# Down projection of an expert layer from the f32 product, in place of two f16 halves of it

## The chip, the cores and the metric

One core of a Trainium2 chip. The metric is the device time in microseconds, median of the runs. The engines are PE (TensorE), DVE (VectorE), ACT (ScalarE), POOL (GpSimd) and SP (SyncE); SP and POOL mostly issue DMAs here, each from a queue of its own that runs in order.

## The reference

Eight rows (batch entries) of 512 tokens with 128 features. Attention with a sine in place of the softmax, 16 heads of 8, then a mixture of experts: one shared expert and eight routed ones, two of which each token uses.

```python
x = x + attention(layernorm(x))            # logits/scale, sin(30 * logits), times V, times Wo
h = layernorm(x)
expert(h, Wg, Wu, Wd) = (silu(h @ Wg.T) * (h @ Wu.T)) @ Wd.T      # 128 -> 256 -> 128
out = x + expert(h, shared) + sum over the top 2 of 8 of score * expert(h, e)
```

All arrays are f32.

## The kernel before

The program is a hand-written order of *slots*, numbered a. Rows 0 to 7 of attention take 32 slots each (0 to 255); from slot 256 (`TAIL`) on only expert work is left, up to slot 331. Each engine runs its own loop over the slots and does in each slot what `plan()` and the slot lists give it. In a slot of attention PE computes the scores of two heads (`scores`), in even slots it multiplies sines with the values (`sum_values`), and ACT takes the sine (`sine`). The projections of the next row and the transposes of the last one lie in slots of their own.

Expert work comes in 148 *tiles* of 128 tokens: 32 *shared* ones, 84 *sparse* ones (tokens of rows 0 to 6 sorted by expert, in four groups of rows, g = 0 to 3) and 32 *full* ones (row 7, each expert over all its tokens). Below slot 256 a tile starts every second slot, after it in every slot. A tile i goes through these steps:

- `gate_up` on PE at `GU_SLOT`: 12 f16 matmuls of 128x128 (high and low halves of weights and tokens, three products for each of four blocks). Up to tile 79 they write the one bank `g_ps`, and so wait for `hidden` of the tile before; later there are three banks.
- `silu` on ACT and `hidden` on DVE at `HID_SLOT` (one slot later, from slot 256 on the same slot). `hidden` writes `hid` in f32 and then casts it to `hid_hi` in f16.
- `hidden_lo` on POOL in the same slot: `hid` minus `hid_hi`, to `hid_lo` in f16.
- `down` on PE at `D_SLOT`, 6 slots after `GU_SLOT` (4 from slot 254 on): 6 f16 matmuls of 128x128 after a wait for `hid_lo`. In a slot PE does `down` before `gate_up`.
- `read_down` on DVE in the same slot, ahead of that slot's `hidden`. A shared or full tile is added to `x_all`. A sparse tile is copied to one of three `y_sb`, which waits for the store of the sparse tile three before, and SP stores it (`store_y`) one slot later.

POOL has the scatters and gathers too. `scatter` sends the tokens of a group to `x_sorted` (16 DMAs for a group of two rows, one a slot, from slots 91, 155, 219; 8 from slot 251). `gather` fetches the results from `y_sorted`, again one DMA a slot, from slots 174, 238, 288 and 318; the first of a group waits until every y of the group is stored. Ten slots after the first gather DVE's `combine` adds the first row of the group (slots 184, 248, 298, 328); the second follows eight slots later or more.

SP's loop does for a slot first `load_rows` (a DMA transpose for a sparse tile, five tiles ahead at most), then `load_weights` (384 KB for a sparse tile, six ahead at most), `load_full` (the weights of an expert for row 7; two buffers, so it waits for the last `down` of the expert two before), then `store_y`, and then the loads and stores of queries and keys. For groups 1 and 2 the first five `load_rows` lie in slots 172 and 236 and wait for the group's scatters; the last y of the group before (tiles 34 and 65) is stored by SP in these same slots, behind them.

The weights are split once at the start (`weights_hi` on POOL, `split_weights` on DVE), stored to `w_dram` and fetched from there.

Of the kernel before, what the change touches and what calls it, by code (L numbers as in the profile page):

```python
# [7 lines left out]
ALU = mybir.AluOpType  # L8
ACT = mybir.ActivationFunctionType
AX = mybir.AxisListType  # L10
F32 = mybir.dt.float32
# [4 lines left out]
P = 128  # L16
# [35 lines left out]
WCOLS = 2 * HID + CH * DM  # L52
TO_WHOLE = 1.5 * 2.0 ** 23
# [35 lines left out]
WR, WF, XT, HR, HB = 6, 2, 5, 5, 6  # L89
# [49 lines left out]
def down_slots():  # L139
    out = []  # L140
    for a in GU_SLOT:
        a = a + 6 if a < TAIL - 2 else a + 4
        out.append(max(a, out[-1]) if out else a)
    return out
# [112 lines left out]
def sine_attention_moe_kernel(nc, x, wq, bq, wk, bk, wv, bv, wo, bo, wgu, wd, wr, rb, ident, out):  # L257
    with ExitStack() as ctx:
# [12 lines left out]
        def dram(name, shape, dt):  # L271
# [34 lines left out]
        w_shared = sb("w_shared", [P, 2 * WCOLS], F16)  # L306
        w_ring = [sb(f"w_ring{i}", [P, 2 * WCOLS], F16) for i in range(WR)]
        w_full = [sb(f"w_full{i}", [P, 2 * WCOLS], F16) for i in range(WF)]
# [3 lines left out]
        hid_hi = [sb(f"hid_hi{i}", [P, HID], F16) for i in range(HB)]  # L312
        hid_lo = [sb(f"hid_lo{i}", [P, HID], F16) for i in range(HB)]
# [24 lines left out]
        w_dram = dram("w_dram", (ROUTED, P, 2 * WCOLS), F16)  # L338
# [28 lines left out]
        gu_done, gate_ready, hid_ready, hid_hi_ready, hid_lo_ready, down_done, d_read = (  # L367
            sem(n) for n in ("gu_done", "gate_ready", "hid_ready", "hid_hi_ready", "hid_lo_ready", "down_done", "d_read"))
# [176 lines left out]
        def _(pe):  # L545
# [116 lines left out]
            def gate_up(i):  # L662
# [7 lines left out]
                else:  # L670
# [7 lines left out]
                    hi, lo = (x2_t[row % 2][:, half * SEQ + t * P:half * SEQ + (t + 1) * P] for half in range(2))  # L678

# [5 lines left out]
                for c in range(2 * CH):  # L685
                    here = bank[:, c * P:(c + 1) * P]
                    w_hi, w_lo = w[:, c * P:(c + 1) * P], w[:, WCOLS + c * P:WCOLS + (c + 1) * P]
# [5 lines left out]
            def down(i):  # L693
# [5 lines left out]
                pe.wait_ge(hid_lo_ready, i + 1)  # L699
# [4 lines left out]
                here = d_bank(i)  # L704
                for c in range(CH):
                    hi, lo = (half[i % HB][:, c * P:(c + 1) * P] for half in (hid_hi, hid_lo))
                    col = 2 * HID + c * DM
                    w_hi, w_lo = w[:, col:col + DM], w[:, WCOLS + col:WCOLS + col + DM]
                    pe.matmul(here, hi, w_hi, start=(c == 0), stop=False)  # L709
                    pe.matmul(here, hi, w_lo, start=False, stop=False)  # L710
                    mm = pe.matmul(here, lo, w_hi, start=False, stop=(c == CH - 1))  # L711
# [164 lines left out]
        def _(dve):  # L876
# [190 lines left out]
            def hidden(i):  # L1067
                dve.wait_ge(gate_ready, i + 1)
                if i >= HR:
                    dve.wait_ge(hid_lo_ready, i - HR + 1)  # L1070
# [275 lines left out]
```

## Time and profile before

| | us |
|---|---|
| median of 3 runs | 589.16 (585.47 to 592.48) |
| the profiled execution | 589.47 |
| its span | 587.6 |
| attention slots, up to slot 256 | about 447 |
| experts alone, from there to the end | about 140 |

The mean granted clock of PE is 0.919 of full speed. Busy time is the time in which an engine had an instruction of its own under way; waits and DMA issues on SP's and POOL's queues are read from the timelines and from the chain that ended last.

### The profile page before, as it was taken

What the parts mean: (1) busy time and instruction counts of PE and PEld (TensorE: products, weight loads), DVE (VectorE), ACT (ScalarE), POOL (GpSimd) and SP (SyncE); (2) the same over time, 40 slices, a digit from 0 to 9 for tenths busy, and PEclk for the clock granted to TensorE, in tenths of its full rate; (3) what the DMA queues carried; (4) which work ended last, traced back from release to release, by engine and by line L of the source; (5) the groups of instructions that cost most, each with busy time, mean ns of one, the idle gap of its engine ahead of it and who ended that gap; (6) DMA issues with size and microseconds to landing.
All of it is one profiled execution on the core that took longest, in us unless ns stands there. A gap on an engine that the chain in (4) does not pass through costs nothing.

```text
span 587.6 us, 13375 instructions
## 1 busy us (share of the span) xinstructions
PE 462.9 (79%) x4616; PEld 244.4 (42%) x4616; DVE 293.9 (50%) x1040; ACT 327.7 (56%) x455; POOL 259.3 (44%) x317
## 2 busy tenths in 40 slices
PE   3298997998969799889876998789758778666761
PEld 2121233233324344444432444344334777565760
DVE  5424444236324446474634555435454865557852
ACT  2279897797856577567643766656734212221220
POOL 4512212003831322168376322357277733388663
PEclk9689999899989999899977999979978879989986
DMA  2889798162718767874397769933645866677322
GB/s 68 240 205 273 234 294 223 64 171 71 240 41 200 181 201 183 243 208 129 80 227 184 178 187 250 183 110 99 131 117 162 198 167 176 188 222 205 99 63 54
DMA packets 101715, 99.14 MB, mean 169 GB/s; under 512 B 32272, under 2 KB 82832, under 8 KB 101648
## 3 DMA queue, kind: packets, MB, share of 16 engines
q1 hardware_dynamic: 95376, 88.91, 56.6%
q0 software_dynamic: 3584, 7.35, 4.9%
q10 hardware_dynamic: 2688, 2.03, 1.2%
q8 instruction: 37, 0.61, 0.5%
q14 instruction: 30, 0.25, 0.2%
HBM read 60.63 MB, written 32.11 MB: 158 GB/s over the span
## 4 chain that ended last, share of the span: by engine, by line
PE 26%; issue 16%; DMA 15%; POOL 15%; SPq 13%; DVE 10%; ACT 5%; ACTq 1%; POOLq 0%; DVEq 0%
PE o_ps L606 6%; PE score L593 5%; SPq L447 5%; POOL x_sorted L1252 5%; POOL y_back L1263 5%; DMA y_sorted<-y_sb 4%; POOL hid_lo L1244 3%; DVE hid L1071 3%; DMA w_ring<-w_dram 3%; PE g_ps L688 2%; DVE x_all L1108 2%; ACT gate L811 2%; PE g_ps L690 2%; PE g_ps L689 2%; SPq L420 2%
## 5 line engine op out<-in xcount | busy, mean ns | idle before, releaser
L790 ACT ACTIVATE attn<-score 128x1024 f32<-128x1024 f32 x256 | 256.4, 1026 | 133.9 <-PE score L593 131.2
L1244 POOL TENSOR_TENSOR hid_lo<-hid,hid_hi 128x256 f16<-128x256 f32 x148 | 102.4, 693 | 204.2 <-DVE hid_hi L1076 203.3
L606 PE MATMUL o_ps<-attn,vals 128*32 128x512 f32 x1024 | 143.3, 633 | 0.1
L593 PE MATMUL score<-queries,keys 64*128 64x512 f16 x512 | 101.7, 404 | 16.2 <-DMA queries<-q_four 9.4
L1071 DVE SCALAR_TENSOR_TENSOR hid<-g_ps,gate 128x256 f32<-128x256 f32 x103 | 43.4, 422 | 128.2 <-ACT gate L811 122.1
L593 PEld LDWEIGHTS score<-queries,keys 64*128 64x128 f16 x512 | 23.9, 93 | 138.9 <-issue 74.6
L688 PE MATMUL g_ps<-xt,w_ring 128*128 128x128 f16 x256 | 51.1, 232 | 24.7 <-DVE hid L1071 10.8
L811 ACT ACTIVATE gate<-g_ps 128x256 f32<-128x256 f32 x103 | 39.2, 381 | 37.7 <-PE g_ps L690 28.6
L689 PE MATMUL g_ps<-xt,w_ring 128*128 128x128 f16 x256 | 51.2, 233 | 0.0
L690 PE MATMUL g_ps<-xt,w_ring 128*128 128x128 f16 x256 | 51.1, 233 | 0.0
L1076 DVE CAST hid_hi<-hid 128x256 f16<-128x256 f32 x148 | 47.3, 320 | 5.1
L811 ACT ACTIVATE gate<-score 128x256 f32<-128x256 f32 x45 | 17.3, 384 | 55.8 <-PE score L690 40.4
L688 PEld LDWEIGHTS g_ps<-xt,w_ring 128*128 128x128 f16 x256 | 26.8, 105 | 31.7 <-issue 27.6
L709 PE MATMUL d_ps<-w_ring,hid_hi 128*128 128x128 f16 x122 | 25.3, 231 | 17.8 <-POOL hid_lo L1244 8.9
L606 PEld LDWEIGHTS o_ps<-attn,vals 128*32 128x32 f32 x1024 | 20.7, 110 | 33.7 <-issue 31.7
L1228 POOL TENSOR_TENSOR rstd<-var_eps,minus_half 128x4 f32<-128x4 f32 x16 | 17.5, 1095 | 27.2 <-DVE var_eps L891 14.8
L1086 DVE COPY y_sb<-d_ps 128x128 f32<-128x128 f32 x61 | 17.3, 283 | 22.7 <-DMA y_sorted<-y_sb 15.7
L690 PEld LDWEIGHTS g_ps<-xt,w_ring 128*128 128x128 f16 x256 | 26.9, 105 | 0.0
L689 PEld LDWEIGHTS g_ps<-xt,w_ring 128*128 128x128 f16 x256 | 26.8, 105 | 0.0
L688 PE MATMUL g_ps<-x_t,w_shared 128*128 128x128 f16 x112 | 20.8, 223 | 7.0 <-DVE hid L1071 7.0
L709 PEld LDWEIGHTS d_ps<-w_ring,hid_hi 128*128 128x128 f16 x122 | 12.2, 100 | 32.0 <-issue 21.7
L711 PE MATMUL d_ps<-w_ring,hid_lo 128*128 128x128 f16 x122 | 25.0, 228 | 0.0
(219 smaller groups left out, 988.9 us busy)
## 6 DMA issues: line engine op xcount, KB each, us to landing
w_ring<-w_dram SPq DMA_DIRECT2D x84, 384.0 KB, 3.3
y_sorted<-y_sb SPq DMA_DIRECT2D x84, 64.0 KB
k_four<-k_minus SPq DMA_DIRECT2D x16, 256.0 KB
q_four<-q_parts SPq DMA_DIRECT2D x14, 256.0 KB
queries<-q_four SPq DMA_DIRECT2D x14, 256.0 KB
keys<-k_four SPq DMA_DIRECT2D x14, 256.0 KB
w_dram<-w_ring SPq DMA_DIRECT2D x8, 384.0 KB, 3.9
w_full<-w_dram SPq DMA_DIRECT2D x8, 384.0 KB, 4.0
```

Of the source, the lines that this page charges most:

```text
L447: sync.dma_start_transpose(xt[r % XT][:, :, :], x_sorted[g % 2][tile * P:(tile + 1) * P, :]).then_inc(xt_loaded[r % XT], 16)
L593: mm = pe.matmul(score[h][:, i, :], keys[b % 2][rows, 2 * j + h, kt * P:(kt + 1) * P], queries[b % 2][rows, 2 * j + h, :], start=True, sto ...
L606: mm = pe.matmul(o_ps[32 * i:32 * i + 32, :], vals[b % 2][:, kt, h:h + 32], attn[k % RING][:, i, :], start=(k == 0), stop=(k == UNITS - 1))
L688: pe.matmul(here, w_hi, hi, start=True, stop=False)
L689: pe.matmul(here, w_hi, lo, start=False, stop=False)
L690: mm = pe.matmul(here, w_lo, hi, start=False, stop=True)
L709: pe.matmul(here, hi, w_hi, start=(c == 0), stop=False)
L790: act.activation(attn[k % RING][:, 2 * (u % 2):2 * (u % 2) + 2, :], score[u % 2][:, :, :], ACT.Sin, scale=SIN_SCALE).then_inc(sined, 1)
L811: act.activation(gate[i % 2][:, :], gu_bank(i)[:, 0:HID], ACT.Silu, scale=UNSCALE).then_inc(gate_ready, 1)
L1071: dve.scalar_tensor_tensor(out=hid[i % HR][:, :], in0=gu_bank(i)[:, HID:2 * HID], scalar=UNSCALE * HSCALE, in1=gate[i % 2][:, :], op0=ALU. ...
L1076: dve.tensor_copy(hid_hi[i % HB][:, :], hid[i % HR][:, :]).then_inc(hid_hi_ready, 1)
L1244: pool.tensor_tensor(hid_lo[i % HB][:, :], hid[i % HR][:, :], hid_hi[i % HB][:, :], ALU.subtract).then_inc(hid_lo_ready, 1)
```

## The change

`hid_hi` and `hid_lo` are gone, with the cast on DVE, the subtraction on POOL and their semaphores. `down` is two f32 matmuls with the f32 `hid` and f32 weights, and waits for `hid` itself. `hid` has six buffers and its next writer waits for `down`. The down weights are held in f32 (scaled by DVE), the gate and up weights as before in two f16 halves in the same buffers; a tile's weights stay 384 KB. `D_SLOT` is 4 slots after `GU_SLOT` (two tiles), from slot 254 on 3. All that hangs on `D_SLOT` moves with it: `store_y`, `load_weights` and `load_full` by two slots (one after slot 256), the first gathers to 172, 236, 287 and 317 and the combines to 182, 246, 297 and 327. `load_rows` stays.

```diff
--- before.py
+++ after.py
@@ -50,6 +50,8 @@
 UNSCALE = 1.0 / (XSCALE * WSCALE)
 DOWN_UNSCALE = 1.0 / (HSCALE * WSCALE)
 WCOLS = 2 * HID + CH * DM
+
+GUCOLS = 2 * HID
 TO_WHOLE = 1.5 * 2.0 ** 23
 
 
@@ -86,7 +88,7 @@
 GTILES = [2 * TT * len(rows) + ROUTED - 1 for rows in ROUTE_GROUPS]
 MAXT = max(GTILES)
 MAXN = TT * max(len(rows) for rows in ROUTE_GROUPS)
-WR, WF, XT, HR, HB = 6, 2, 5, 5, 6
+WR, WF, XT, HR = 6, 2, 5, 6
 BANKS = 3
 
 
@@ -139,7 +141,7 @@
 def down_slots():
     out = []
     for a in GU_SLOT:
-        a = a + 6 if a < TAIL - 2 else a + 4
+        a = a + 4 if a < TAIL - 2 else a + 3
         out.append(max(a, out[-1]) if out else a)
     return out
 
@@ -303,14 +305,12 @@
 
         x_pack = [sb(f"x_pack{i}", [P, TT, 2 * DM], F16) for i in range(4)]
         x2_t = [sb(f"x2_t{i}", [P, 2 * SEQ], F16) for i in range(2)]
-        w_shared = sb("w_shared", [P, 2 * WCOLS], F16)
-        w_ring = [sb(f"w_ring{i}", [P, 2 * WCOLS], F16) for i in range(WR)]
-        w_full = [sb(f"w_full{i}", [P, 2 * WCOLS], F16) for i in range(WF)]
+        w_shared = sb("w_shared", [P, WCOLS])
+        w_ring = [sb(f"w_ring{i}", [P, WCOLS]) for i in range(WR)]
+        w_full = [sb(f"w_full{i}", [P, WCOLS]) for i in range(WF)]
         xt = [sb(f"xt{i}", [P, 2, P], F16) for i in range(XT)]
         gate = [sb(f"gate{i}", [P, HID]) for i in range(2)]
         hid = [sb(f"hid{i}", [P, HID]) for i in range(HR)]
-        hid_hi = [sb(f"hid_hi{i}", [P, HID], F16) for i in range(HB)]
-        hid_lo = [sb(f"hid_lo{i}", [P, HID], F16) for i in range(HB)]
         y_sb = [sb(f"y_sb{i}", [P, DM]) for i in range(3)]
         y_back = sb("y_back", [P, MAXN * 2, DM])
         stage = [y_back[:, :, :].rearrange("p t n -> p (t n)")[:, i * WCOLS:(i + 1) * WCOLS] for i in range(2)]
@@ -335,7 +335,7 @@
 
         q_three, k_three = (dram(n, (P, 3, SEQ), F16) for n in ("q_three", "k_three"))
         q_four, k_four = (dram(n, (P, 4, SEQ), F16) for n in ("q_four", "k_four"))
-        w_dram = dram("w_dram", (ROUTED, P, 2 * WCOLS), F16)
+        w_dram = dram("w_dram", (ROUTED, P, WCOLS), F32)
         x_sorted = [dram(f"x_sorted{i}", (MAXT * P, 2 * DM), F16) for i in range(2)]
         y_sorted = [dram(f"y_sorted{i}", (MAXT * P, DM), F32) for i in range(2)]
 
@@ -364,8 +364,8 @@
             sem(n) for n in ("ranked", "pos_ready", "place_step", "places_ready", "experts_ready", "shares_ready"))
         cleared, scattered, gathered = sem("cleared"), sem("scattered"), sems("gathered", 2)
         xt_loaded, w_loaded, f_loaded, y_stored = sems("xt_loaded", XT), sems("w_loaded", WR), sems("f_loaded", WF), sems("y_stored", 3)
-        gu_done, gate_ready, hid_ready, hid_hi_ready, hid_lo_ready, down_done, d_read = (
-            sem(n) for n in ("gu_done", "gate_ready", "hid_ready", "hid_hi_ready", "hid_lo_ready", "down_done", "d_read"))
+        gu_done, gate_ready, hid_ready, down_done, d_read = (
+            sem(n) for n in ("gu_done", "gate_ready", "hid_ready", "down_done", "d_read"))
         half_summed, combined, out_stored = sem("half_summed"), sem("combined"), sem("out_stored")
 
         def x_row(b):
@@ -676,6 +676,7 @@
                         pe.wait_ge(w_split, 1)
                         w = w_shared
                     hi, lo = (x2_t[row % 2][:, half * SEQ + t * P:half * SEQ + (t + 1) * P] for half in range(2))
+                w = w[:, 0:GUCOLS].bitcast(F16)
 
                 if i >= GU_MAIN + BANKS - 1:
                     pe.wait_ge(hid_ready, i - BANKS + 1)
@@ -684,7 +685,7 @@
                 bank = gu_bank(i)
                 for c in range(2 * CH):
                     here = bank[:, c * P:(c + 1) * P]
-                    w_hi, w_lo = w[:, c * P:(c + 1) * P], w[:, WCOLS + c * P:WCOLS + (c + 1) * P]
+                    w_hi, w_lo = w[:, c * P:(c + 1) * P], w[:, GUCOLS + c * P:GUCOLS + (c + 1) * P]
                     pe.matmul(here, w_hi, hi, start=True, stop=False)
                     pe.matmul(here, w_hi, lo, start=False, stop=False)
                     mm = pe.matmul(here, w_lo, hi, start=False, stop=True)
@@ -696,19 +697,15 @@
                     w = w_ring[RANK[i] % WR]
                 else:
                     w = w_full[e % WF] if kind == FULL else w_shared
-                pe.wait_ge(hid_lo_ready, i + 1)
+                pe.wait_ge(hid_ready, i + 1)
                 if i >= D_MAIN + BANKS - 1:
                     pe.wait_ge(d_read, i - BANKS + 1)
                 elif i:
                     pe.wait_ge(d_read, min(i, D_MAIN))
                 here = d_bank(i)
+                w_down = w[:, GUCOLS:]
                 for c in range(CH):
-                    hi, lo = (half[i % HB][:, c * P:(c + 1) * P] for half in (hid_hi, hid_lo))
-                    col = 2 * HID + c * DM
-                    w_hi, w_lo = w[:, col:col + DM], w[:, WCOLS + col:WCOLS + col + DM]
-                    pe.matmul(here, hi, w_hi, start=(c == 0), stop=False)
-                    pe.matmul(here, hi, w_lo, start=False, stop=False)
-                    mm = pe.matmul(here, lo, w_hi, start=False, stop=(c == CH - 1))
+                    mm = pe.matmul(here, hid[i % HR][:, c * P:(c + 1) * P], w_down[:, c * DM:(c + 1) * DM], start=(c == 0), stop=(c == CH - 1))
                 mm.then_inc(down_done, 1)
 
 
@@ -948,7 +945,9 @@
             def split_weights(e):
                 dve.wait_ge(w_hi_ready, e + 1)
                 mine = w_ring[(e - 1) % WR] if e else w_shared
-                dve.scalar_tensor_tensor(out=mine[:, WCOLS:], in0=stage[e % 2], scalar=WSCALE, in1=mine[:, 0:WCOLS],
+                dve.tensor_scalar(mine[:, GUCOLS:], stage[e % 2][:, GUCOLS:], WSCALE, None, ALU.mult)
+                mine = mine[:, 0:GUCOLS].bitcast(F16)
+                dve.scalar_tensor_tensor(out=mine[:, GUCOLS:2 * GUCOLS], in0=stage[e % 2][:, 0:GUCOLS], scalar=WSCALE, in1=mine[:, 0:GUCOLS],
                                          op0=ALU.mult, op1=ALU.subtract).then_inc(w_split, 1)
 
             def residual(j):
@@ -1067,13 +1066,9 @@
             def hidden(i):
                 dve.wait_ge(gate_ready, i + 1)
                 if i >= HR:
-                    dve.wait_ge(hid_lo_ready, i - HR + 1)
+                    dve.wait_ge(down_done, i - HR + 1)
                 dve.scalar_tensor_tensor(out=hid[i % HR][:, :], in0=gu_bank(i)[:, HID:2 * HID], scalar=UNSCALE * HSCALE, in1=gate[i % 2][:, :],
                                          op0=ALU.mult, op1=ALU.mult).then_inc(hid_ready, 1)
-                dve.wait_ge(hid_ready, i + 1)
-                if i >= HB:
-                    dve.wait_ge(down_done, i - HB + 1)
-                dve.tensor_copy(hid_hi[i % HB][:, :], hid[i % HR][:, :]).then_inc(hid_hi_ready, 1)
 
             def read_down(i):
                 kind, row, t, e = TILES[i]
@@ -1237,11 +1232,7 @@
                 if e - 1 >= WR:
                     pool.wait_ge(w_stored, 16 * (e - 1))
                 mine = w_ring[(e - 1) % WR] if e else w_shared
-                pool.tensor_scalar(mine[:, 0:WCOLS], stage[e % 2], WSCALE, 1.0, ALU.mult, ALU.mult).then_inc(w_hi_ready, 1)
-
-            def hidden_lo(i):
-                pool.wait_ge(hid_hi_ready, i + 1)
-                pool.tensor_tensor(hid_lo[i % HB][:, :], hid[i % HR][:, :], hid_hi[i % HB][:, :], ALU.subtract).then_inc(hid_lo_ready, 1)
+                pool.tensor_scalar(mine[:, 0:GUCOLS].bitcast(F16)[:, 0:GUCOLS], stage[e % 2][:, 0:GUCOLS], WSCALE, 1.0, ALU.mult, ALU.mult).then_inc(w_hi_ready, 1)
 
             def scatter(g, row, t, c):
                 j = ROUTE_GROUPS[g][row]
@@ -1296,8 +1287,6 @@
             add_bo(1)
             for a in range(END + 1):
                 b, s = divmod(a, SLOTS)
-                for i in HID_AT.get(a, ()):
-                    hidden_lo(i)
                 if 1 <= b < ROWS and s == S_POW2:
                     inv_sqrt(b - 1, 1)
                 if a - TAIL == E_POW2:
```

## Rows read from the trace of the kernel before

**Rows 1.** The page, part 1: busy us, share of the span, instructions of each engine.

```profile
PE 462.9 (79%) x4616; PEld 244.4 (42%) x4616; DVE 293.9 (50%) x1040; ACT 327.7 (56%) x455; POOL 259.3 (44%) x317
```

**Rows 2.** Groups by line: out<-in, shapes, count | busy us, mean ns | idle before, releaser.

```profile
L1244 POOL TENSOR_TENSOR hid_lo<-hid,hid_hi 128x256 f16<-128x256 f32 x148 | 102.4, 693 | 204.2 <-DVE hid_hi L1076 203.3
L1076 DVE CAST hid_hi<-hid 128x256 f16<-128x256 f32 x148 | 47.3, 320 | 5.1
```

**Rows 3.** Waits of PE, 260 to 455 us: us in total, times, longest us.

```profile
PE d_ps L709 <- DVE y_sb L1086: 11.5, 3, 4.4
PE d_ps L709 <- POOL hid_lo L1244: 6.0, 2, 3.2
```

**Rows 4.** Timeline of POOL in a gather burst: start us, duration us, instruction, idle before.

```profile
310.10 0.68 POOL L1244 TENSOR_TENSOR hid_lo<-hid,hid_hi 128x256 f16<-128x256 f32 x1
310.94 0.96 POOL L1263 DMA_INDIRECT y_back<-y_sorted,place0a  x1 [0.16 <-issue]
312.20 0.94 POOL L1263 DMA_INDIRECT y_back<-y_sorted,place0b  x1 [0.30 <-issue]
```

**Rows 5.** Timeline of DVE: two long waits that held it.

```profile
312.88 1.14 DVE L1108 SCALAR_TENSOR_TENSOR x_all<-y_back,share0a,x_all 128x128 f32<-128x128 f32 x4 [6.50 <-DMA y_back<-y_sorted,place0b]
...
383.80 0.29 DVE L1086 COPY y_sb<-d_ps 128x128 f32<-128x128 f32 x1 [5.85 <-DMA y_sorted<-y_sb]
```

**Rows 6.** Timeline of PE and DVE, one tile in a clean stretch.

```profile
190.03 0.23 PE L709 MATMUL d_ps<-w_ring,hid_hi 128*128 128x128 f16 x1
190.15 0.42 DVE L1071 SCALAR_TENSOR_TENSOR hid<-g_ps,gate 128x256 f32<-128x256 f32 x1 [2.15 <-ACT gate L811]
190.31 0.22 PE L711 MATMUL d_ps<-w_ring,hid_lo 128*128 128x128 f16 x1
190.72 0.22 PE L688 MATMUL g_ps<-xt,w_ring 128*128 128x128 f16 x1 [0.18 <-DVE hid L1071]
```

**Rows 7.** f32 matmuls of 128x128, L619: one timeline row; durations min/median/max ns.

```profile
69.14 1.16 PE L619 MATMUL r_ps<-wo_s,o_t 128*128 128x128 f32 x8
...
L619 PEld LDWEIGHTS r_ps<-wo_s,o_t x64: 186/192/192, 69.1 to 456.8; 128*128 128x128 f32 x64
```

**Rows 8.** Timeline of DVE: hid of tiles 22, 38, 54, 69 and 76.

```profile
227.54 0.42 DVE L1071 SCALAR_TENSOR_TENSOR hid<-g_ps,gate 128x256 f32<-128x256 f32 x1 [0.49 <-ACT gate L811]
...
285.89 0.42 DVE L1071 SCALAR_TENSOR_TENSOR hid<-g_ps,gate 128x256 f32<-128x256 f32 x1 [0.49 <-ACT gate L811]
...
355.30 0.42 DVE L1071 SCALAR_TENSOR_TENSOR hid<-g_ps,gate 128x256 f32<-128x256 f32 x1 [0.94 <-ACT gate L811]
...
411.71 0.42 DVE L1071 SCALAR_TENSOR_TENSOR hid<-g_ps,gate 128x256 f32<-128x256 f32 x1 [1.28 <-ACT gate L811]
...
447.39 0.42 DVE L1071 SCALAR_TENSOR_TENSOR hid<-g_ps,gate 128x256 f32<-128x256 f32 x1 [2.04 <-ACT gate L811]
```

**Rows 9.** Timeline of SyncE's queue (SPq), first and last issues of the full stretch.

```profile
456.99 1.19 SPq L447 DMA_TRANSPOSE xt<-x_sorted  x1
...
491.09 1.21 SPq L447 DMA_TRANSPOSE xt<-x_sorted  x1
494.08 1.20 SPq L447 DMA_TRANSPOSE xt<-x_sorted  x1
...
540.68 0.34 SPq L457 DMA_DIRECT2D w_ring<-w_dram  x1
```

**Rows 10.** Timeline of ACT: the silu of the last sparse tile.

```profile
550.74 0.38 ACT L811 ACTIVATE gate<-score 128x256 f32<-128x256 f32 x1 [0.54 <-PE score L690]
```

**Rows 11.** Chain that ended last, 540 us to the end: start us, us, what.

```profile
557.48 2.90 issue
...
566.18 2.36 issue
```

**Rows 12.** Timeline of DVE, the last us.

```profile
572.93 0.41 DVE L1071 SCALAR_TENSOR_TENSOR hid<-g_ps,gate 128x256 f32<-128x256 f32 x1
...
581.13 1.13 DVE L1108 SCALAR_TENSOR_TENSOR x_all<-y_back,share3b,x_all 128x128 f32<-128x128 f32 x4
```

## The prediction

> **What bounds the kernel now.** I read the page first, then the waits, then the timelines of each engine where a wait was long, and last the chain. No engine is full: PE is busy 79% of the span, POOL 44% [rows 1]. So the bound differs from stretch to stretch, and there are four.
>
> (1) Slots 0 to 112 hold hardly any tiles; they are loads, sines and scores, and the change touches almost nothing there.
>
> (2) The clean part of the attention slots with tiles. A tile takes 3.1 us, and the loop that closes is `gate_up`, scores, sine, silu, `hidden`, next `gate_up` (they share the one bank). The reader is to see that `down` is beside this loop: its six matmuls start every 0.056 us (190.03 to 190.31), so PE is through by 190.37, and `gate_up` starts at 190.72, released by DVE's `hid` [rows 6]. PE has 0.35 us of slack in such a tile.
>
> (3) The bursts of gathers. POOL's queue runs in order, and two gathers at 1.27 us with a `hidden_lo` at 0.84 (310.10 to 310.94) make 3.1 us for two slots, the whole of what a tile takes [rows 4]. A burst that starts late never catches up: DVE waits 6.50 us in `combine` for gathers [rows 5], PE stands before `down` for `hid_lo` and for `y_sb` [rows 3], and everything in order behind them stands too.
>
> (4) After slot 256. From 456.99 to 540.68 the SP queue issues almost without a gap: a sparse tile costs it 494.08 - 491.09 = 2.99 us (the transpose, two register reads, a weight load, a store), for two tiles of the plan [rows 9]. Behind that come 47 us with combines, waits for full weights (2.90 and 2.36 us in the chain) [rows 11] and an end in which `down` and the last combine wait for POOL.
>
> **The change part by part.** The sum is made against the span of 587.6; the run around it took 589.47, 0.3 above the median.
>
> *PE's work.* Six f16 matmuls (6 x 0.056 = 0.33 us) become two f32 ones, which the trace shows as two instructions each. The projections L619 have this very shape: eight instructions in 1.16 us, of which the last takes about 0.275 to drain, so one starts every 0.126 us [rows 7]. A `down` takes 4 x 0.126 = 0.50, that is +0.17 us. In a clean tile of (2) it fits into the slack of 0.35. It is paid where PE is the later one: about 3 tiles of 16 in a row, those behind a projection in an even slot, so 13 tiles x 0.17 = 2.2, and some at the low clock; I take +4. Bounds: 0, and 78 tiles x 0.17 = 13. The f32 weight load takes 0.192 us [rows 7], but within those eight instructions it lay beside the matmuls. The Trainium skill (TensorE: Matmul & The Clock Gate, Weight-path perf modes) says that the fast weight load is off for FP32; the 0.192 agrees in direction. By loads that hide behind nothing `down` would be 4 x 0.192 = 0.77, +0.44 a tile; the cadence of the row says it isn't so, and the sum goes by the row.
>
> *Cast and subtraction.* DVE loses 0.32 us a tile and POOL 0.69 [rows 2]. In (2) both are cover, worth nothing: `hid_lo` is ready slots before `down` needs it. They count where POOL is late.
>
> *The bursts in the attention slots.* With no `hidden_lo` in its queue POOL issues a gather every 1.27 us against 1.55 us for a slot. And `store_y` of tiles 34 and 65 moves from slots 172 and 236 to 170 and 234, ahead of the five transposes that wait for the scatters; today it is issued behind them. The first row's eight gathers then take 8 x 1.27 = 10.2, plus some 2.5 to land, 8 slots from slot 172, and the combine is at 182. Price of group 0: tile 38 to tile 54 is 32 slots and takes 355.30 - 285.89 = 69.4; tile 22 to 38 is the same 32 slots a row and a half-turn earlier and takes 58.4 [rows 8]: -11. Group 1: tile 69 to 76 (16 slots) takes 35.7; tile 54 to the tile at 384.00, the same phase a row earlier, takes 28.7 [rows 5, 8]: -7. That 28.7 holds itself a wait of 5.85 for a store of y, queued on SP next to the keys' loads, which costs 3.7; the store gets ahead of those loads by the two slots, and I count half: -2. Together -20. Bounds: 0 if the wait only changes its name, -24 with all of it.
>
> *The stretch of the SP queue.* Its work isn't changed: 24 transposes with their loads and stores at 2.99 are 71.8, with four loads of full weights and two stores of rows some 74 of the 83.7 us [rows 9]. The rest, 9 to 10, is waiting for DVE or PE; most of it is the combine of group 2, whose gathers pace it at 1.8 us each with a `hidden_lo` between. I take -6 (0 to -9). The beginning, where `rstd` stands behind a `hidden_lo`, -1.
>
> *The end*, from the last `w_ring` issue at 540.68. The last sparse tile is reached some 5.4 us sooner (its silu is at 550.74 [rows 10], 10.1 us after that issue, kept by the combine; a load of 3.5 and `gate_up` with its waits, 1.2, are needed). Then PE is the bound, at 12 x 0.056 + 0.50 = 1.17 a tile for 0.98 today: about +0.5 in each of three blocks of four to six tiles. The two waits for full weights [rows 11]: today one tile's work lies beside a load of some 3.5 us, with `down` a tile nearer two lie beside it, so 2.9 and 2.4 become some 1.5: -2.7; a stretch at the low clock behind the first goes with it, -1. After the last `hid` (572.93) DVE ends at 582.26, 9.3 us later [rows 12], as POOL has hidden_lo's and gathers to do. Afterwards POOL has run ahead, `down` follows at once, and DVE has left three reads of 0.3 and two combines of 1.13: 3.3 to 3.7, -5.7. Sum -5.4 + 1.5 - 2.7 - 1 - 5.7 = -13.3. Bounds -8 and -17.
>
> *Waits that are added.* `hidden` waits for the `down` of six tiles before; `down` is two or three tiles behind, so it is free. `down` waits for `hid` of two tiles before, ready a slot and more ahead. Queued behind PE's wait would be `gate_up`, and ACT and DVE behind that. `split_weights` gets one more DVE operation and shorter others, long before the weights are used: nothing.
>
> *Sum:* +4 - 20 - 6 - 1 - 13.3 = -36.3. 587.6 - 36.3 = 551.3 of span, with 1.9 around it 553.
>
> **The rivals.**
>
> *A, the waits change their name* (chance 0.20). SP's queue is full after slot 256, and DVE still waits there for stores of y that take some 4 us to land; in the attention slots the gathers of group 0 now run into the loads of queries. Then the bursts give back half (-10), the stretch 0, the end -9, PE +4: -15 to -20, 566 to 575. For it: the 5.85 us are a DMA wait and not POOL's [rows 5]. Against: of the 6.50 the queue of POOL explains all.
>
> *B, PE becomes the bound and it is slower* (0.05). One mechanism: f32 weight loads that don't hide between f16 neighbours. With load and matmul one behind the other `down` costs 4 x (0.192 + 0.275) = 1.87, +1.54 on 148 tiles less the slack of 0.35 in some 65: +205, less the 40 gained, about 750. The sign turns where `down` costs about 0.33 + 0.35 + 40/148 = 0.95 us, twice what the projections show. By the page's rule alone, 0.77, it would be +0.09 on clean tiles and +0.44 where PE is the bound, some 25 of the 40 lost, 575.
>
> *C, more is gained* (0.12). Half the low-clock stretches follow the bursts, and with fewer of them PE keeps 2.4 GHz; SP's queue never waits: -9 there, -24 in the bursts, -17 at the end, PE +2: -48, 541 and below.
>
> *D, nothing happens* (0.05): the gathers' landing and not POOL's queue holds the combines, the SP queue sets the rest, and +13 on PE eats what is left: 583 to 595.
>
> **How the numbers follow.** The forecast has 0.58, its own range 543 to 566. The range is to leave out 2 in 10: all of B (0.05), D (0.05), a quarter of A and some 0.05 of C. That gives 538 to 575. A measurement of this kernel can tell about 1% from no change, so faster is below 583.3: forecast, A and C, 0.90. Same is D's larger part, 0.04. Slower is B and the rest of D, 0.06.
>
> **What would show it.** Interval from tile 38's `hid` to tile 54's: 58 instead of 69. No wait of PE for `y_sb` above 2 us below slot 256. Four `down` instructions in 0.50 us. 3.1 us for a clean tile. SP's stretch about 77 us and still without gaps. POOL's last gather long before the last `hid`, and 4 us from that `hid` to DVE's last combine. I am wrong in the terms of the bursts if `combine` waits longer than 2 us for its gathers, and in PE's if clean tiles take 3.3 us.

## The result, and the profile after

| | us |
|---|---|
| before, six runs | 587.95 (585.47 to 592.48) |
| after, six runs | 634.07 (632.0 to 638.68) |
| after / before | 1.0781, 95% interval 1.0738 to 1.0823 |
| forecast | 553 (538 to 575) |
| profiled execution of after, its span | 636.7 |

The kernel became 46 us slower. The page of after, its busy times (part 1) and its chain by engine (part 4), in the columns of [rows 1]:

```profile
PE 489.3 (77%) x4320; PEld 267.0 (42%) x4320; DVE 231.6 (36%) x901; ACT 328.8 (52%) x455; POOL 151.5 (24%) x169
...
PE 41%; issue 16%; SPq 15%; DMA 9%; another core or an unknown queue 8%; DVE 5%; ACT 4%; ACTq 1%; POOL 0%; DVEq 0%; POOLq 0%
```

DVE lost 62 us of work and POOL 108 (47 and 102 of them are the cast and the subtraction of [rows 2]). PE has 26 us more than before and is busy 77% of a longer span, for 79%. What is new is "another core or an unknown queue" in the chain of a program that has one core: 8% of 636.7 us is about 51 us, near the 46 us lost. The waits of after over the whole span say where it sits (us in total, times, longest us; "remote" is the same: the profile finds no releaser). The trace of before has no such row. (SyncE's queue has four such waits in after, 42 us together.)

```profile
ACT attn L787 <- remote: 62.8, 10, 18.2
...
DVE x_all L1090 <- remote: 25.9, 7, 7.0
ACT gate L808 <- remote: 25.4, 3, 10.6
```

By the code these three lines wait for the semaphores `scored`, `down_done` and `gu_done`, all of them PE's. The timelines of PE, ACT, DVE and POOL around the longest one (start us, duration us, instruction, idle before it):

```profile
297.03 0.39 PE L593 MATMUL score<-queries,keys 64*128 64x512 f16 x2
...
315.10 0.61 PE L593 MATMUL score<-queries,keys 64*128 64x512 f16 x2 [16.38 <-ACT attn L787]
...
294.76 1.02 ACT L787 ACTIVATE attn<-score 128x1024 f32<-128x1024 f32 x1 [0.42 <-remote]
314.02 1.02 ACT L787 ACTIVATE attn<-score 128x1024 f32<-128x1024 f32 x1 [18.24 <-remote]
...
297.61 0.29 DVE L1090 SCALAR_TENSOR_TENSOR x_all<-d_ps,x_all 128x128 f32<-128x128 f32 x1 [2.29 <-remote]
...
295.48 0.94 POOL L1254 DMA_INDIRECT y_back<-y_sorted,place0b  x1 [0.30 <-issue]
...
310.48 0.94 POOL L1254 DMA_INDIRECT y_back<-y_sorted,place0b  x1 [0.30 <-issue]
```

The reader is to see that PE has finished the scores of 297.03 by 297.42, and that ACT takes them up at 314.02. (The view models the ends of matmuls; but PE starts the next tile's `down` at 298.04, behind the scores in its order. And the sine has a second wait, for `sum_values` of an older slot, which is PE's too.) From 300.8 us on PE waits for ACT, DVE for both, SyncE's queue issues nothing, and only POOL works: it issues 18 indirect DMAs in a row, from 288.9 to 311.4, one in 1.25 us, with nothing between them. ACT goes on 2.6 us after the last. The others are of the same kind: in each stretch in which POOL had eight or more indirect DMAs in a row, ACT stood 4 to 18 us at a time, and mostly went on 2 to 4 us behind the last of them.

Set against a kernel without these waits (one of the experiments below, e18, span 536.5), the time from the start to tile 38 is 36 us longer, tile 38 to 54 2, 54 to 69 25, 69 to 76 17, 76 to 133 12, 133 to 146 8, and the end the same: 100 us, the difference of the spans.

### The profile page after: what moved, and what is told of

The parts are those of the page before. It is cut to its first block, busy times and chain, and to the rows that moved or that the text cites. A ratio compares the mean times of both kernels' runs of the same rounds, so it can differ in the third digit from the quotient of the medians.

```text
span 636.7 us, 12353 instructions
## 1 busy us (share of the span) xinstructions
PE 489.3 (77%) x4320; PEld 267.0 (42%) x4320; DVE 231.6 (36%) x901; ACT 328.8 (52%) x455; POOL 151.5 (24%) x169
## 4 chain that ended last, share of the span: by engine, by line
PE 41%; issue 16%; SPq 15%; DMA 9%; another core or an unknown queue 8%; DVE 5%; ACT 4%; ACTq 1%; POOL 0%; DVEq 0%; POOLq 0%
PE o_ps L606 10%; PE score L593 7%; SPq L447 6%; DMA y_sorted<-y_sb 6%; PE d_ps L708 5%; PE g_ps L689 3%; PE g_ps L691 3%; PE g_ps L690 2%; SPq L456 2%; ACT attn L787 2%; SPq L457 2%; PE score L708 2%; SPq L476 2%; DMA keys<-k_four 1%
## 5 line engine op out<-in xcount | busy, mean ns | idle before, releaser
L689 PE MATMUL g_ps<-xt,w_ring 128*128 128x128 f16 x256 | 48.8, 226 | 18.7 <-DVE hid L1070 16.4
L708 PE MATMUL d_ps<-w_ring,hid 128*128 128x128 f32 x248 | 44.4, 302 | 8.0 <-DVE y_sb L1081 5.4
L690 PE MATMUL g_ps<-xt,w_ring 128*128 128x128 f16 x256 | 48.9, 227 | 0.0
L691 PE MATMUL g_ps<-xt,w_ring 128*128 128x128 f16 x256 | 48.8, 226 | 0.0
L708 PEld LDWEIGHTS d_ps<-w_ring,hid 128*128 128x128 f32 x248 | 32.9, 193 | 21.0 <-issue 19.4
L689 PEld LDWEIGHTS g_ps<-xt,w_ring 128*128 128x128 f16 x256 | 25.9, 101 | 25.6 <-issue 21.5
L690 PEld LDWEIGHTS g_ps<-xt,w_ring 128*128 128x128 f16 x256 | 25.9, 101 | 0.4
L691 PEld LDWEIGHTS g_ps<-xt,w_ring 128*128 128x128 f16 x256 | 26.1, 102 | 0.0
L1070 DVE SCALAR_TENSOR_TENSOR hid<-score,gate 128x256 f32<-128x256 f32 x45 | 18.8, 418 | 19.0 <-issue 10.3
L708 PE MATMUL score<-w_full,hid 128*128 128x128 f32 x84 | 16.3, 314 | 9.7 <-issue 6.7
L708 PE MATMUL d_ps<-w_shared,hid 128*128 128x128 f32 x112 | 21.3, 316 | 1.6 <-issue 1.0
```

The costliest lines, as they stand in the source:

```text
L689: pe.matmul(here, w_hi, hi, start=True, stop=False)
L690: pe.matmul(here, w_hi, lo, start=False, stop=False)
L691: mm = pe.matmul(here, w_lo, hi, start=False, stop=True)
L708: mm = pe.matmul(here, hid[i % HR][:, c * P:(c + 1) * P], w_down[:, c * DM:(c + 1) * DM], start=(c == 0), stop=(c == CH - 1))
L1070: dve.scalar_tensor_tensor(out=hid[i % HR][:, :], in0=gu_bank(i)[:, HID:2 * HID], scalar=UNSCALE * HSCALE, in1=gate[i % 2][:, :], op0=ALU. ...
```

## The experiments

They ran in groups, each on one chip and with the kernel before beside it. The chips may matter, so they have letters here, in the order in which the groups ran. Which chips the six runs of before and of after had isn't known, nor whether their two traces come from one chip.

| chip | kernel before, us | kernels | longest "remote" wait in each, us |
|---|---|---|---|
| A | 594.53 (590.8 to 594.79) | e1, e2, e3, e4 | 4.7, 11.6, 5.7, 16.3 |
| B | 586.45 (583.41 to 589.77) | e5, e6, e7, e8 | none in any |
| C | 592.55 (590.19 to 598.71) | e9, e10, e11, e12 | 18.3, 16.2, 12.4, 8.0 |
| D | 586.04 (582.73 to 587.35) | e13 to e15 | none in any |
| D | 584.86 (two runs) | e16 to e18 | none in any |

**Chip A: which part of the change does it?** The four edits, shortened (e3 has a semaphore of its own around the subtraction, e4 two unused semaphores):

```diff
e1, of before
-        a = a + 6 if a < TAIL - 2 else a + 4
+        a = a + 4 if a < TAIL - 2 else a + 3
e2, of after: the same line the other way round
e3, of after
+                pool.wait_ge(hid_ready, i + 1)
+                pool.tensor_tensor(pace_out[:, :], pace_in[:, :], pace_in[:, :], ALU.subtract)   # once a tile
e4, of after
+        unused = [sb(f"unused{i}", [P, HID]) for i in range(5)]
```

> The kernel before with one line of the change alone: down follows by two tiles (slot + 4, in the tail + 3), with the f16 halves and POOL's subtraction kept. The trace of after has waits of ACT of up to 18.24 us (314.02) that fall into runs of up to 18 gathers with nothing between them on POOL. Theory 1 (an unbroken run of indirect DMAs on POOL holds back PE's completions at the other engines; the change made the runs long by taking hidden_lo out): the subtraction still breaks the runs, so no such waits, 580 to 590 us. Theory 2 (it is the moved slots: gathers, stores of y and transposes now meet in another order): the waits are there, 615 to 640. Theory 3 (the f32 matmuls) and theory 4 (buffers and semaphores lie elsewhere): no waits, as theory 1.

> The changed kernel with down put back to its old slots (+ 6, in the tail + 4); f32 down, no halves, no subtraction on POOL. Theory 1: POOL's queue holds gathers alone as in after, the waits of ACT for PE stay, 615 to 640 us. Theory 2 (moved slots): the waits are gone, 560 to 590. Theories 3 and 4: waits as in after, 615 to 640.

> The changed kernel with POOL's subtraction put back as a dummy: once a tile POOL waits for hid_ready and subtracts one scratch buffer from itself into f16 (128x256); nobody waits for the result, down is f32 and follows by two tiles. Theory 1: the runs of indirect DMAs are broken and paced by the tiles again, the waits of ACT for PE above 5 us are gone, and the rest of the change (down not waiting for POOL, the slots) is left: 555 to 590 us. Theories 2, 3 and 4: the waits stay, 615 to 640.

> The changed kernel with five unused buffers of 1 KB a partition and two unused semaphores in the places of those that the change removed, so that what follows keeps its address and number; nothing else. Theory 4 (the place of buffers or the number of a semaphore decides; it would explain why the first ten scatters, at 150 to 164 us, came with no wait before and with one after, though the program is the same there): the waits are gone, 553 to 590 us. Theories 1, 2 and 3: as after, 625 to 640.

Measured: e1 578.77 (ratio 0.9754, 0.961 to 0.9897, so not clearly 2% faster), e2 635.02 (1.0702), e3 573.38 (0.9663, 0.9543 to 0.9783), e4 639.56 (1.0778). Old slots and the old layout change nothing; a wait for the tile and a subtraction on POOL, whose result nobody reads, bring over 60 us. e2's timeline of ACT and e3's waits show it:

```profile
408.30 1.02 ACT L787 ACTIVATE attn<-score 128x1024 f32<-128x1024 f32 x1 [10.47 <-remote]
```

```profile
DVE x_all L1092 <- remote: 11.0, 3, 5.7
...
ACT attn L789 <- remote: 9.9, 5, 4.7
```

So on this chip the cause is settled as far as the program goes: PE's signals come late once POOL's queue no longer has a tile's subtraction, and the wait for the tile, between its indirect DMAs. Which of the two helps, the subtraction or the wait that spreads the DMAs over the tiles, isn't told apart: the wait alone (e5) ran on another chip. Nor is POOL's own work on an indirect DMA told apart from the traffic that it starts. e3 and e1 still have short waits of this kind, all but one beside the ten scatters from 149 us or a run of four. Slots, f32 and layout are out as causes.

**Chip B: what has to stand between them?** The edits of e5 to e8, shortened:

```diff
e5, of after: once a tile
+                pool.wait_ge(hid_ready, i + 1)
e6, of after: behind each indirect DMA
+                pool.memset(idle[:, k:k + 1], 0.0)
e7, of after: behind every second one
+                pool.tensor_tensor(pace_out[:, :], pace_in[:, :], pace_in[:, :], ALU.subtract)
e8, of before
-            for k, slot in enumerate(GATHER_SLOT[g]) if slot == a]
+            for k in range(SCATTERS[g]) if GATHER_SLOT[g][k - k % (2 * TT)] == a]
```

> The changed kernel plus one thing: once a tile POOL waits for hid_ready of that tile, and computes nothing there. The run before this one with wait and subtraction took 573 us and had single waits of ACT of 5 us at most apart from the first runs. Theory 1a (what holds PE's signals back is many indirect DMAs close together; a wait on the tile spreads them to two in 3.1 us): 565 to 580 us, no wait of ACT marked remote above 5 us in the attention slots. Theory 1b (it takes another instruction of POOL, with its 0.84 us, between them): a wait on a semaphore that is long up lets POOL run on, the runs of indirect DMAs stay long where POOL is late, 600 to 635.

> The changed kernel with a memset of one element a partition on POOL behind each of the 112 indirect DMAs; no wait is added. One indirect DMA starts every 1.25 us in the trace of after; with the memset that should be about 1.35. Theory 1a (density in time): almost as after, 615 to 635 us, the waits of up to 18 us stay. Theory 1b (any other instruction between two of them breaks the effect): the waits are gone, 555 to 585.

> The changed kernel with a 128x256 subtraction of scratch data on POOL behind every second indirect DMA, which waits for no tile: two gathers and a subtraction take about 3.4 us, as in the bursts of the kernel before, but unpaced. Theory 1a: density falls from one in 1.25 us to one in 1.7, the long waits are gone, 560 to 590 us. Theory 1c (it is not the density but POOL's running free, ahead of the tiles and against the SP queue's transposes and loads): still 610 to 635.

> The kernel before, with all eight gathers of a row issued in the slot of its first one, so that eight stand in POOL's queue with no hidden_lo between them; every other slot as before. Theory 1: waits of ACT marked remote appear in the kernel before too, some 4 to 6 us in each of the seven runs of eight (the ten scatters of after cost 4.7), and the hidden_lo behind the run is up to 7 us late; 600 to 630 us. Theories 2 to 4, by which f32, buffers or slots of down are needed: no such waits, only the late hidden_lo, 590 to 605.

Measured: e5 544.32, e6 539.60 (0.920, 0.906 to 0.9339), e7 547.84, e8 596.28 (1.0166, 1.0014 to 1.0318, so hardly apart from before). For a while I read this as: any instruction between two indirect DMAs is the cure, even a memset of 0.12 us that leaves the cadence at 1.25. But e5 has a run of ten and e8 one of ten and seven of eight, and neither has a "remote" wait. What e8 lost is late subtractions (PE waits 39.7 us for `hid_lo` in all, 18.3 in before), as this row of PE shows:

```profile
304.27 0.29 PE L709 MATMUL d_ps<-w_ring,hid_hi 128*128 128x128 f16 x1 [7.21 <-POOL hid_lo L1244]
```

Ten of the 16 scatters of group 0 give the cleanest comparison between the chips, for they stand in a row in e1 to e5, e8, e9, before and after, and little that the edits touch comes ahead of them. Each of e1 to e4 and e9 has waits marked "remote" beside them, e5 and e8 none. ACT in e4, and the last of the ten on POOL, with ACT, in e5:

```profile
158.91 1.02 ACT L788 ACTIVATE attn<-score 128x1024 f32<-128x1024 f32 x1 [5.74 <-remote]
```

```profile
158.51 0.96 POOL L1243 DMA_INDIRECT x_sorted<-x_pack,place0b  x1 [0.30 <-issue]
...
159.37 1.02 ACT L787 ACTIVATE attn<-score 128x1024 f32<-128x1024 f32 x1 [0.15 <-PE score L593]
```

**Chip C: the border.** Behind each indirect DMA e9 has `pool.wait_ge(consts, 3)`, a semaphore that has long been up, and for which the view has no instruction between the DMAs (POOL has 169 in e9 as in after); e10 has e6's memset behind every fourth, e11 behind every eighth, and e12 is the kernel before with e6's memset behind each.

> The changed kernel with one more wait on POOL behind each indirect DMA, for a semaphore (consts) that has been at its value since the first 20 us; nothing is computed. With a memset of 0.12 us there the time was 540 us, with one gather still starting every 1.25 us. Theory 1b (any other instruction in POOL's queue between two indirect DMAs is enough): 540 to 550 us, no waits marked remote. Theory 1d (it takes an instruction that POOL's processing part executes and finishes; a wait is handled by its sequencer): as after, 625 to 640, with waits of 10 to 18 us.

> The changed kernel with the memset of one column behind every fourth indirect DMA only, so that the longest run is four. In the trace of after, the waits begin 2 to 8 us into a run, the second to seventh DMA of it. If something has to fill up first (theory 1e, a threshold above four): 540 to 545 us and no long wait. If each DMA that follows another directly costs its share: a part of the 94 us between 634 and 540 comes back, with runs of four some 20 to 40 us, 560 to 580.

> The same with the memset behind every eighth indirect DMA, runs of eight. By theory 1e with a threshold of four to six: waits marked remote of up to 5 us in the 14 runs, 555 to 590 us. If the waits need runs longer than eight (the runs of 14 to 18 in after are the costly ones): 540 to 550.

> The kernel before, unchanged but for the memset of one column behind each of the 112 indirect DMAs. Its trace has no wait marked remote, and the subtraction stands between every two gathers. By theory 1 the memsets do nothing for it and cost POOL 0.1 us each where it is late: 585 to 597 us. If the same effect also holds the kernel before back, unseen (its four gathers in a row at 296 us and 422 us, its ten scatters), the time falls to 560 to 580, and part of what the memset gave the changed kernel is not the change's.

Measured: e9 637.67 (1.077), e10 638.15 (1.0778), e11 644.38 (1.0883), e12 593.77 (0.9996, 0.9941 to 1.0052). The waits are those of after, in e10 too, with runs of four. And e12 has them although a memset stands between every two of its indirect DMAs. One of DVE, 5.2 us up to 314.31, falls among gathers with memset and subtraction between the pairs. The longest of ACT falls behind the scatters; ACT and POOL:

```profile
165.13 1.94 ACT L791 ACTIVATE attn<-score 128x1024 f32<-128x1024 f32 x2 [6.90 <-remote]
...
160.93 0.96 POOL L1261 DMA_INDIRECT x_sorted<-x_pack,place0a  x1 [0.19 <-issue]
161.88 0.12 POOL L1233 MEMSET idle<- 128x1 f32 x1
162.19 0.95 POOL L1261 DMA_INDIRECT x_sorted<-x_pack,place0b  x1 [0.19 <-issue]
```

So the memset isn't a safe cure here, the subtraction isn't a complete one, and the reading of chip B was in doubt.

**Chip D: the parts of the gain, and the run by itself.** e13 is e6 with the old slots; e14 has the memset behind every second DMA, e16 behind every third; e15 is e6 with the instructions of `down` issued twice; e17 has a plain `dma_start` of the same size for each indirect one (it leaves out the sorting of the tokens, so its output isn't the reference's); e18 is e6 without the memset in the 16 gathers of group 0.

```diff
e15
-                for c in range(CH):
+                for c in list(range(CH)) * 2:
e18
+                if not 32 <= k < 48:
+                    pool.memset(idle[:, k:k + 1], 0.0)
```

> The changed kernel with the memset of one column behind each indirect DMA and with down at its old slots (+ 6, in the tail + 4). With the new slots the same kernel takes 540 us. My sum gave the slots the y store ahead of the transposes, the earlier combine and about half of the end. If the slots matter: 548 to 560 us. If the gain is all POOL's freed queue: 539 to 545.

> The changed kernel with the memset of one column behind every second indirect DMA, so that they come in pairs, still one in 1.25 us. If the number in a row decides (pairs with a subtraction of 0.69 us were harmless, 548 us; fours with a memset were not, 638): 539 to 546 us, no wait marked remote above 3 us. If it is the time that POOL is off indirect DMAs (0.12 us in 2.5 would be too little): 590 to 640.

> The changed kernel with the memset behind each indirect DMA, and with the four instructions of down issued twice (the same result written again), eight in place of four. The difference to 540 us is what 4 x 0.126 = 0.50 us more on PE a tile costs, 74 us of work over 148 tiles. By my step (clean tiles in the attention slots have some slack, after slot 256 PE is the bound in part of the tiles): 565 to 585 us, that is 0.3 to 0.6 of it on the path; f32 for three f16 matmuls (+0.17 a tile) then costs a third of the difference, 8 to 15 us. If PE is hidden nearly everywhere: 545 to 555, and f32 costs 2 to 5 us, near the +4 of the forecast.

> The changed kernel with the memset of one column behind every third indirect DMA. Pairs take 539 us, fours 638. If the border is at three in a row: 620 to 645 us. If it is at four: 537 to 545. If it is gradual: in between, with fewer or shorter waits marked remote than with fours.

> The changed kernel without any memset, in which each of the 112 indirect DMAs is a plain DMA of the same size (128 rows, one tile of 128 rows in DRAM in place of the scattered ones), still from POOL's queue; the tokens are therefore not sorted by expert and the output is not the reference's. If it takes POOL's own work on an indirect DMA (0.95 us each, back to back): no waits marked remote, 525 to 545 us. If the traffic behind it or POOL's queue full of DMAs is enough: the waits stay, 600 to 640.

> The changed kernel with the memset of one column behind each indirect DMA except the 16 gathers of group 0, which stand in one unbroken run as in after (there from 288.9 to 311.4 us with the last two scatters, with one wait of ACT of 18.2 us). With all memsets the time is 540 us. Theory 1 (the run itself is what stops the others): one or two waits of ACT marked remote within that run, 12 to 20 us in all, and 552 to 560 us. If the effect needs what other runs leave behind (a backlog, the low clock): 538 to 543.

Measured: e13 555.72 (0.9492), e14 539.37 (0.9225, 0.9182 to 0.9268), e15 565.05, e16 543.93, e17 535.10, e18 537.03 (0.9182, 0.9086 to 0.9278). e18 is the one that overturns my theory. Its POOL issues 16 gathers in one unbroken run, and ACT takes up PE's scores at once all the while:

```profile
275.74 0.99 POOL L1264 DMA_INDIRECT y_back<-y_sorted,place0a  x1 [1.39 <-issue]
...
295.04 0.94 POOL L1264 DMA_INDIRECT y_back<-y_sorted,place0b  x1 [0.30 <-issue]
...
290.03 0.39 PE L594 MATMUL score<-queries,keys 64*128 64x512 f16 x2
...
293.13 0.39 PE L594 MATMUL score<-queries,keys 64*128 64x512 f16 x2
...
293.56 1.02 ACT L788 ACTIVATE attn<-score 128x1024 f32<-128x1024 f32 x1 [0.75 <-PE score L594]
```

Scores that start at 293.13 are read at 293.56, with the fourteenth of the 16 gathers beside them. In the same stretch ACT stood 18.2 us in after. "A long run stops the others" is false as a general rule.

**What holds, and what stays open.** One reading fits all 18 traces whose chip is known: it takes two things, a run of indirect DMAs in POOL's queue and something that chips A and C (and the one on which after was measured) have and B and D have not. All eight kernels of A and C have "remote" waits, all ten of B and D have none, whatever their runs; and the kernel before itself takes 592.6 to 594.5 on the first two and 584.9 to 586.5 on the others, about what its ten scatters would cost it (4.7 us in e1's trace, 6.9 in e12's). That is an estimate: the kernel before was not traced on A or C, and its one trace, with prompt signals beside ten scatters, is from a chip that isn't known. Within chip A, e3 and e4 differ in POOL's subtraction with its wait and in unused buffers alone, and by 66 us.

But after itself was run on neither B nor D, and e6, e14 and e18 on neither A nor C. So I can't say that after takes some 540 us on chip B or D, though e18 speaks for it, nor what the memset is worth on A or C; e10 and e12 speak against it. After, e6 and e3 side by side on a chip of each kind would tell. Whether it is the chip or the hour isn't told apart either, though with, without, with and without followed one another, which a slow drift wouldn't do. And why PE's signals and not DVE's or ACT's come late no view shows. The best time of a kernel with the reference's result is 537 to 540 us (e18, e14, e6), on B and D; on a chip that has the effect the best is e3's way, 0.966 of before.

## Why the prediction was wrong, step by step

**The step that failed** is in the bursts: "With no `hidden_lo` in its queue POOL issues a gather every 1.27 us", and in the end: "Afterwards POOL has run ahead". The cadence is right, 1.25 us. I took a freed queue as a gain that only other queues could eat, and had no rival in which POOL's own work is what stops the other engines. Rival B was the only slow one, and it was about PE. Nothing in the trace of before showed the mechanism: its longest run, ten scatters from 151.6 us, came with prompt signals. What a reader could have seen is that the change makes runs which the trace of before doesn't have: its gathers stand in pairs with a subtraction behind each pair [rows 4]. That was an operation the trace doesn't show, and I bounded its cost at zero.

In after itself the terms came out like this, by the same marks as in the table further down: start to tile 38 +29.5 us (forecast -1), 38 to 54 -8.9 (-11), 54 to 76 +26.6 (-9), 76 to the last `w_ring` issue +9.4 (-6), to tile 133 -5.0 (-5.4), to the end -2.5 (-7.9). So the bursts, priced at -20 from tile 38 to tile 76, took 17.7 us more, and the stretch in front of tile 38, which holds the run of 18 DMAs and was priced at -1, took 29.5 us more.

One reading of the forecast was off as well, without harm: two gathers at 1.27 us and a subtraction at 0.84 are 3.38 and not 3.1. The 3.1 is right, for POOL starts the next subtraction right behind the second gather, 3.08 us after the one before:

```profile
307.02 0.68 POOL L1244 TENSOR_TENSOR hid_lo<-hid,hid_hi 128x256 f16<-128x256 f32 x1
...
310.10 0.68 POOL L1244 TENSOR_TENSOR hid_lo<-hid,hid_hi 128x256 f16<-128x256 f32 x1
```

**PE's work: right in the mechanism and near in size.** Timelines of PE and DVE of after, a clean tile, beside [rows 6]:

```profile
192.49 0.71 PE L708 MATMUL d_ps<-w_ring,hid 128*128 128x128 f32 x4
...
193.18 0.22 PE L689 MATMUL g_ps<-xt,w_ring 128*128 128x128 f16 x1
...
192.61 0.42 DVE L1070 SCALAR_TENSOR_TENSOR hid<-g_ps,gate 128x256 f32<-128x256 f32 x1 [2.18 <-ACT gate L808]
...
195.71 0.43 DVE L1070 SCALAR_TENSOR_TENSOR hid<-g_ps,gate 128x256 f32<-128x256 f32 x1 [1.40 <-ACT gate L808]
```

The tile still takes 3.10 us. Behind slot 256, where PE is the bound, the forecast was 12 x 0.056 + 0.50 = 1.17:

```profile
592.75 0.42 DVE L1070 SCALAR_TENSOR_TENSOR hid<-score,gate 128x256 f32<-128x256 f32 x1 [0.55 <-ACT gate L808]
...
593.92 0.42 DVE L1070 SCALAR_TENSOR_TENSOR hid<-score,gate 128x256 f32<-128x256 f32 x1 [0.49 <-ACT gate L808]
...
595.09 0.42 DVE L1070 SCALAR_TENSOR_TENSOR hid<-g_ps,gate 128x256 f32<-128x256 f32 x1 [0.55 <-ACT gate L808]
```

It is 1.17 to the digit, so the weight loads hide. e15 says what the term is worth. Twice the f32 instructions make a PE-bound tile 1.62 and a clean one 3.40. So one more `down` costs 0.45 where PE is the bound, and 0.30 in a clean tile, where 0.15 of slack is left. e15's span is 28.1 us longer than e14's; 17.4 of them lie before tile 76, 10.0 between 76 and 146 and 0.7 behind. In the clean tiles the first 0.17 is free; behind 76 it costs an estimated 0.17 / 0.45 x 10.0 = 3.8. In front of 76 the tiles behind a projection take the full 0.45 in e15 (4.54 and 4.40 us for 4.10 and 3.95), so there some of the forecast's 2.2 us for them may come on top. That makes 4 to 6, by estimate; the forecast had +4. My expectation of e15, a third of the difference, was too simple: the cost isn't a straight line.

**The gains, where the waits are absent.** e6 (span 539.6, on chip B) against the trace of before; `hid` of tiles 38, 54, 69 and 76 in e6, as [rows 8] has them for before:

```profile
281.26 0.42 DVE L1071 SCALAR_TENSOR_TENSOR hid<-g_ps,gate 128x256 f32<-128x256 f32 x1 [1.17 <-issue]
...
340.41 0.42 DVE L1071 SCALAR_TENSOR_TENSOR hid<-g_ps,gate 128x256 f32<-128x256 f32 x1 [1.08 <-ACT gate L809]
...
391.91 0.42 DVE L1071 SCALAR_TENSOR_TENSOR hid<-g_ps,gate 128x256 f32<-128x256 f32 x1 [1.96 <-ACT gate L809]
...
417.25 0.42 DVE L1071 SCALAR_TENSOR_TENSOR hid<-g_ps,gate 128x256 f32<-128x256 f32 x1 [2.18 <-ACT gate L809]
```

| stretch | before | e6 | difference | forecast |
|---|---|---|---|---|
| start to tile 38 | 285.9 | 281.3 | -4.6 | -1 |
| 38 to 54 | 69.4 | 59.2 | -10.3 | -11 |
| 54 to 76 | 92.1 | 76.8 | -15.2 | -9 |
| 76 to the last `w_ring` issue | 93.3 | 91.1 | -2.2 | -6 |
| to the last sparse tile (133) | 11.3 | 6.4 | -4.9 | -5.4 |
| 133 to the end | 35.6 | 24.8 | -10.8 | -7.9 |
| PE, spread over all | | | in the above | +4 |
| sum | 587.6 | 539.6 | -48.0 | -36.3 |

Tile 38 to 54 was forecast at 58 us; it takes 59.2 here and 60.5 in after itself. From the last `hid` to the end of the last combine I said 3.3 to 3.7 us; in e6 it is 533.46 to 536.76, 3.3. So the mechanisms that I priced are there, in sum a third larger than priced, and near rival C's -48. One of C's reasons is there, the granted clock, 0.966 over the span against 0.919 before; but its stretch of the SP queue gave -2.2 and not -9. The trace of before may be from another chip than e6's; beside e6, on chip B, the kernel before took 586.45 us.

**Whose gain it is.** I split the bursts between POOL's queue and the slots without a test; I wrote of the wait of 6.50 in `combine` [rows 5] that "the queue of POOL explains all". e13, with POOL free but the old slots, has it still; its waits of PE and DVE:

```profile
PE d_ps L709 <- DVE y_sb L1082: 10.8, 4, 5.5
...
DVE x_all L1104 <- DMA y_back<-y_sorted,place0b: 7.1, 2, 6.7
```

In e14, with the new slots, no combine of group 0 waits that long, and the first row is this:

```profile
PE d_ps L709 <- DVE y_sb L1082: 4.1, 5, 2.0
```

The slots are worth 16 us (555.7 against 539.4; e14 has half the memsets, and e6 with all of them took 539.6), 4.9 of them between tiles 38 and 54 and 6.9 between 69 and 76. e1 says the same on chip A: the slots alone, with POOL's subtraction kept, bring 16 us (590.8 to 594.79 against 575.91 and 581.63).

**The rivals.** A (waits change their name) didn't come; B was excluded by the 1.17; C is what e6, e14 and e18 show; D isn't it. The result was none of them.

## What to carry to other kernels

An operation that goes away from a queue also took time between its neighbours. Before counting that as a gain, write out what now stands back to back there and ask whether the trace has ever shown such a run; if it hasn't, keep a price for it on both sides. And run the kernels that are to be compared on one chip: here relatives of after came out near 540 us on two chips and near 640 on the two others, none of them was run on both kinds, and the kernel before moved by 1.6% only.

## What the runs showed of the hardware

- PE's completions can reach ACT, DVE and SyncE's queue up to 18 us late while POOL issues indirect DMAs one in 1.25 us, and mostly come through 2 to 4 us after the last. The view shows it as "remote" or "an unknown queue". On two of four chips none of ten kernels had it, even with 16 gathers in a row; on the two others all eight had it, one of them with runs of four at most (up to 16 us), and one with a memset behind every DMA (up to 8 us).
- An f32 matmul of 128x128 costs two instructions of 0.126 us (eight in 1.16 us in e15's `down` as in the projections [rows 7]). Its weight loads of 0.19 us hide also between f16 neighbours, since the PE-bound tile takes 1.17 us. The Trainium skill (TensorE: Matmul & The Clock Gate, Weight-path perf modes) has the fast weight load off for FP32; the loads are indeed twice as long as the f16 ones (0.196 against 0.099 us in e6's groups), and it cost nothing here.
- On chip D 112 plain DMAs from POOL's queue, 0.53 us each, in place of the indirect ones (0.95 us) gave 535.1 us (534.01 to 536.19) for e18's 537.0 (535.72 to 538.33). So where the signals are prompt, POOL's work on them is worth some 2 us, hardly more than the spread.
